# First attention layer: value products in half units behind a score group, a ring of four turned tiles, and another order of scores, copies and exponentials

## The reference

```
q, k, v = x @ Wq, x @ Wk, x @ Wv
attn = softmax((q @ k^T) * scale)     # per head, 512 x 512
out = (attn @ v) @ Wo
```

## Time and profile before

| what | us |
|---|---|
| median of three runs | 1487.92 |
| lowest, highest | 1484.96, 1489.2 |
| the profiled execution, its own time | 1479.72 |
| span of the profiled execution | 1477.9 |
| PE busy in the span | 1278.4 (87%) |
| DVE, ACT, POOL busy | 1058.7 (72%), 775.1 (52%), 524.5 (35%) |
| first and last score group begin | 21.4, 777.5 |

### The profile page before, as it was taken

How to read it: one execution, slowest core, us unless ns; L and a number is a source line. 1 busy time by engine, 2 the same in 40 slices (tenths; PEclk the granted TensorE clock), 3 DMA queues, 4 the chain that set the end, 5 groups by cost and what they waited for, 6 DMA issues and landing times. The chain is left out here.

```text
span 1477.9 us, 22423 instructions
## 1 busy us (share of the span) xinstructions
PE 1278.4 (87%) x8226; PEld 640.0 (43%) x8226; DVE 1058.7 (72%) x1823; ACT 775.1 (52%) x1308; POOL 524.5 (35%) x434
## 2 busy tenths in 40 slices
PE   4777788777877787877888899999999999999998
PEld 2232333232322233322333355585548654765466
DVE  6688877666766567656777498687878688669846
ACT  5676666554655557545661775236533554246532
POOL 2389853002210022100221156323733274317531
PEclk9899999998999999999999999999999999999999
DMA  7775545565555665565657502300230111210221
GB/s 242 187 168 99 92 91 90 105 123 104 92 104 98 130 114 98 106 119 114 112 102 227 212 20 55 86 16 29 55 71 23 37 45 43 55 37 19 55 48 44
DMA packets 346557, 135.52 MB, mean 92 GB/s; under 512 B 312176, under 2 KB 333392, under 8 KB 343888
## 3 DMA queue, kind: packets, MB, share of 16 engines
q1 hardware_dynamic: 334032, 132.52, 40.6%
q10 hardware_dynamic: 12416, 1.57, 1.0%
HBM read 44.87 MB, written 17.87 MB: 42 GB/s over the span
## 5 line engine op out<-in xcount | busy, mean ns | idle before, releaser
L929 ACT ACTIVATE probs<-vpair,top_n 128x512 f16<-128x512 f32 x256 | 164.4, 687 | 256.3 <-DVE top_n L627 256.3
L1143 PE MATMUL bank<-rows,both 128*128 128x512 f16 x1024 | 244.7, 392 | 5.2 <-DVE fd L700 4.1
L627 DVE TENSOR_REDUCE top_n<-vpair 128x1 f32<-128x512 f32 x256 | 164.5, 684 | 84.9 <-PE bank L1114 82.8
L443 POOL TENSOR_TENSOR h<-th,h 128x512 f16<-128x512 f32 x61 | 71.5, 1172 | 271.5 <-ACT h L898 271.5
L627 DVE TENSOR_REDUCE top_n<-bank 128x1 f32<-128x512 f32 x256 | 163.7, 681 | 0.0
L929 ACT ACTIVATE probs<-bank,top_n 128x512 f16<-128x512 f32 x256 | 162.6, 690 | 0.0
L1143 PEld LDWEIGHTS bank<-rows,both 128*128 128x128 f16 x1024 | 97.5, 100 | 144.5 <-issue 35.4
L2218 PE MATMUL bank<-rows,both 128*128 128x512 f16 x512 | 118.3, 382 | 0.0
L1114 PE MATMUL vpair<-qk 32*128 32x512 f16 x256 | 50.4, 389 | 74.4 <-ACT probs L929 74.4
L2234 PE MATMUL bank<-both,hid 128*128 128x512 f16 x512 | 111.2, 379 | 0.0
L1128 PE MATMUL bank<-probsT,vaug 128*32 128x512 f16 x512 | 45.3, 487 | 72.3 <-DMA probsT<-probs 60.4
(11 more groups left out here) (362 smaller groups left out, 2673.3 us busy)
## 6 DMA issues: line engine op xcount, KB each, us to landing
h<-in_ug SPq DMA_DIRECT2D x8, 1024.0 KB, 5.8
lt_scratch<-big SPq DMA_DIRECT2D x16, 384.0 KB, 2.7
dn<-in_down SPq DMA_DIRECT2D x2, 2048.0 KB, 11.1
x_scratch<-th SPq DMA_DIRECT2D x16, 256.0 KB, 2.6
res<-x_scratch SPq DMA_DIRECT2D x16, 256.0 KB, 4.1
out_x<-res SPq DMA_DIRECT2D x16, 256.0 KB, 2.0
both<-in_w SPq DMA_DIRECT2D x2, 1548.0 KB, 11.9
t_scratch<-tok SPq DMA_DIRECT2D x16, 192.0 KB, 2.1
```

What stands on the lines that cost most here:

```text
L443: pool.tensor_tensor(h16(ft, 1), row32, h16(ft, 0), ALU.subtract).then_inc(S["row_lo"], 1)
L627: v.tensor_reduce(top_n[:, i:i + 1], SC_[n % G][:, :], AX.X, ALU.max, negate=True).then_inc(S["max_done"], 1)
L929: a.activation(probs[:, k % TAKEN, j * T:(j + 1) * T], SC_[j][:, :], ACT.Exp, bias=top_n[:, i:i + 1]).then_inc(S["p_ready"], 1)
L1143: mm = pe.matmul(GB[n % 2][:, :], w[:, kt, col:col + P], xnb(b, kt), start=r == 0, stop=r == 2 * KT - 1)
```

## The change

- `weigh(n)` now forms the value products of two query tiles, 16 matmuls of 256 columns. It stands at t % 4 == 0, directly behind the score group of that step, and takes the tiles 2n and 2n + 1, whose scores stand eight and six steps before.
- `turn_probs(n)` waits only until the pair that held its quarter of `probsT` has been used: `probsT` becomes a ring of four turned tiles.
- `to_tokens`, `divide` and `to_features` move to the steps 4, 6 and, for the unit before last, 2.
- `load_heads` is split: k rows two units ahead at t % 8 == 6, q rows one unit ahead at t % 8 == 2.
- On PE, `scores` comes behind the turns and transforms of its step, and in the feed-forward stages behind a few of the step's matmuls: 4 or 3 of the gate stage (t % 4 == 0 or 2), 1 or 0 of the down stage.
- On ACT, `high_rows` and `high_half` come ahead of the exponentials of their step; the copies of q, v and k come one step later from t = 70 on.

```
-PV_STEP, TOKEN_STEP, DIVIDE_STEP, TURN_BACK = 2, 3, 4, 6
+TOKEN_STEP, DIVIDE_STEP, TURN_BACK = 4, 6, 2
+GATE_AHEAD, DOWN_AHEAD = (4, 3), (1, 0)
+LATE_EVICT = 70
...
+            def load_q(u):
+
+                slot = u % SLOTS
                 sp.wait_ge(S["mb_took"], MB["q", u // 2] + 1)
+                if u >= SLOTS:
+                    sp.wait_ge(S["s_ps"], (u - SLOTS + 1) * SC)
...
                 sp.wait_ge(S["p_ready"], G * (n + 1))
                 if u:
-                    sp.wait_ge(S["pv_done"], u)
+                    sp.wait_ge(S["pv_done"], n // 2 - 1)
...
-                if t % STEPS == STEPS - 2 and 1 < t // STEPS + 2 < NU:
-                    load_heads(t // STEPS + 2)
+                if t % STEPS == 6 and t // STEPS + 2 < NU:
+                    load_k(t // STEPS + 2)
+                if t % STEPS == 2 and 1 < t // STEPS + 1 < NU:
+                    load_q(t // STEPS + 1)
...
-                if t % STEPS == TURN_BACK and 0 <= t // STEPS - 1 < NU and t // STEPS % 2 == 0:
-                    to_features(t // STEPS - 1)
+                if t % STEPS == TURN_BACK and 0 <= t // STEPS - 2 < NU and t // STEPS % 2:
+                    to_features(t // STEPS - 2)
...
+                if t > FFN_STEP + 1 and (t - 2) // BSTEPS < B and (t - 2) % BSTEPS >= FFN_STEP and t % 2 == 0:
+                    high_rows((t - 2) // BSTEPS, ((t - 2) % BSTEPS - FFN_STEP) // 2)
                 if b < B and m > FFN_STEP and m % 2:
                     tanh_gate(b, (m - FFN_STEP) // 2)
+                if 0 <= t - PREP - 2 < NCH * KT:
+                    high_half(t - PREP - 2)
                 if t < NU * STEPS:
                     exps(2 * t)
                     exps(2 * t + 1)
...
-                if t % 16 == Q_STEP + 1 and t // 16 + 1 < NU // 2:
+                late = 1 if t < LATE_EVICT else 2
+                if t % 16 == Q_STEP + late and t // 16 + 1 < NU // 2:
                     evict_q(t // 16 + 1)
-                if m == K_STEP + 1 and b + 1 < B:
+                if m == K_STEP + late and b + 1 < B:
                     evict_k(b + 1)
...
-            def weigh(u):
-
+            def weigh(n):
+
+                u, half = divmod(n, 2)
                 b, g = divmod(u, NKV)
-                for i in range(TAKEN):
-                    pe.wait_ge(S[f"pt_in{i}"], 16 * ((TT * (u + 1) - 1 - i) // TAKEN + 1))
-                if u:
+                for k in (2 * n, 2 * n + 1):
+                    pe.wait_ge(S[f"pt_in{k % TAKEN}"], 16 * (k // TAKEN + 1))
+                if u and half == 0:
                     pe.wait_ge(S["o_free"], u)
-                if g == 0:
+                if g == 0 and half == 0:
                     pe.wait_ge(S["mb_took"], MB["v", b] + 1)
+                cols = slice(2 * P * half, 2 * P * (half + 1))
                 for kt in range(TT):
                     for j in range(G):
-                        mm = pe.matmul(OB[32 * j:32 * j + 32, :], vaug[:, b % 2, kt, g, :], probsT[:, TT * j + kt, :],
+                        mm = pe.matmul(OB[32 * j:32 * j + 32, cols], vaug[:, b % 2, kt, g, :], probsT[:, TT * j + kt, cols],
                                        start=kt == 0, stop=kt == TT - 1)
                 mm.then_inc(S["pv_done"], 1)
...
+            def ffn(t, first, last):
+
+                b, m = t // BSTEPS, t % BSTEPS
+                if b and m < FFN_STEP:
+                    for i in range(first, min(last, 6)):
+                        down_mm((b - 1) * TT + m // 8, 2 * (m % 8) + i // 3, i % 3)
+                if b < B and m >= FFN_STEP:
+                    for r in range(first, last):
+                        ffn_mm(b, m - FFN_STEP, r)
...
-                if t < NU * STEPS and t % 2 == 0:
-                    scores(t // 2)
-                if t % STEPS == PV_STEP and 0 <= t // STEPS - 1 < NU:
-                    weigh(t // STEPS - 1)
                 if t in TURN_STEP:
                     turn_x(KT + TURN_STEP.index(t))
                 if 0 <= t - PREP - 2 < NCH * KT:
                     transform_ug(t - PREP - 2)
+                ahead = 0
+                if t % 2 == 0:
+                    ahead = (DOWN_AHEAD if m < FFN_STEP else GATE_AHEAD)[t // 2 % 2]
+                ffn(t, 0, ahead)
+                if t < NU * STEPS and t % 2 == 0:
+                    scores(t // 2)
+                if t % 4 == 0 and 0 <= t // 4 - 2 < 2 * NU:
+                    weigh(t // 4 - 2)
+                ffn(t, ahead, 2 * KT)
```

More of the change, by code:

```diff
@@ L298, in _, with load_k @@
             load_chunk(1)
-            def load_heads(u):
+            def load_k(u):
                 b, g, slot = u // NKV, u % NKV, u % SLOTS
@@ L330, in load_raw @@
                 if i == 0:
-                    sp.wait_ge(S["pv_done"], NU)
+                    sp.wait_ge(S["pv_done"], 2 * NU)
                 if i == 2:
@@ L343, in turn_probs @@
                 if u:
-                    sp.wait_ge(S["pv_done"], u)
+                    sp.wait_ge(S["pv_done"], n // 2 - 1)
                 sp.dma_start_transpose(probsT[:, :, qt * P:(qt + 1) * P], probs[:, n % TAKEN, :]).then_inc(S[f"pt_in{n % TAKEN}"], 16)
-            load_heads(0)
-            load_heads(1)
+            for u in range(2):
+                load_k(u)
+                load_q(u)
             sp.dma_start(wsd[:, :], d["wscale_dp"].partition_broadcast(P)).then_inc(S["wo_in"], 16)
@@ L660, in to_tokens @@
             def to_tokens(u):
-                v.wait_ge(S["pv_done"], u + 1)
+                v.wait_ge(S["pv_done"], 2 * (u + 1))
                 if u:
@@ L917, in evict_v @@
                 if b >= 2:
-                    a.wait_ge(S["pv_done"], (b - 1) * NKV)
+                    a.wait_ge(S["pv_done"], 2 * (b - 1) * NKV)
                 a.activation(vaug[:, b % 2, :, :, 0:DH], MISC[:, :].rearrange("p (t g c) -> p t g c", t=TT, g=NKV),
@@ L989, in _ @@
                     evict_x(KT + TURN_STEP.index(t))
-                if 0 <= t - PREP - 2 < NCH * KT:
-                    high_half(t - PREP - 2)
                 for ft in range(FT):
@@ L996, in _ @@
                     high_down(DN_AT.index(t))
-                if t % 16 == Q_STEP + 1 and t // 16 + 1 < NU // 2:
+                late = 1 if t < LATE_EVICT else 2
+                if t % 16 == Q_STEP + late and t // 16 + 1 < NU // 2:
                     evict_q(t // 16 + 1)
-                if m == V_STEP + 1 and b + 1 < B:
+                if m == V_STEP + late and b + 1 < B:
                     evict_v(b + 1)
-                if m == K_STEP + 1 and b + 1 < B:
+                if m == K_STEP + late and b + 1 < B:
                     evict_k(b + 1)
-                if t > FFN_STEP + 1 and (t - 2) // BSTEPS < B and (t - 2) % BSTEPS >= FFN_STEP and t % 2 == 0:
-                    high_rows((t - 2) // BSTEPS, ((t - 2) % BSTEPS - FFN_STEP) // 2)
                 if b and m - 1 in DOWN_END:
@@ L1145, in ffn_mm, with down_mm @@
                     mm.then_inc(S["gb_full"], 1)
-            def down_mm(n, j):
+            def down_mm(n, j, r):
                 k, ft = GO["down", n], DN_TURN[j]
-                if j == 0:
+                if j == 0 and r == 0:
                     pe.wait_ge(S["gb_took"], k - 1)
-                if n % TT == 0:
+                if n % TT == 0 and r == 0:
                     pe.wait_ge(S["row_lo"], n // TT * FT + ft + 1)
-                if n == 0:
+                if n == 0 and r == 0:
                     pe.wait_ge(S["mb_took"], MB["dn", j] + 1)
                 bk, rows = GB[k % 2][:, :], slice(n % TT * P, (n % TT + 1) * P)
[L1157 to L1160, removed]
+                mm = pe.matmul(bk, h16(ft, r // 2)[:, rows], dn16(ft, r % 2), start=j == 0 and r == 0, stop=j == FT - 1 and r == 2)
+                if j == FT - 1 and r == 2:
                     mm.then_inc(S["gb_full"], 1)
+            def ffn(t, first, last):
[6 more added lines that the diff above has]
+                        ffn_mm(b, m - FFN_STEP, r)
             def turn_next():
@@ L1208, in _ @@
                     transform_dn(DN_AT.index(t))
[L1209 to L1214, removed]
                 if t % 16 == Q_STEP and t // 16 + 1 < NU // 2:
```

## The result

The changed kernel takes 1390.93 us (median of four runs, 1388.45 to 1393.41) against 1486.66 of the kernel before (four runs, 1484.96 to 1489.2): a ratio of 0.9355, 95% interval 0.9332 to 0.9378. It is faster by about 96 us; forecast were 108. The profiled execution of before was a low one of its kind (1479.72), that of after (1391.33) a typical one, so the traces show 88.4 us of the difference: 87.1 up to the last score group (777.5 to 690.37), 1.4 behind it.

The account below looks back on a forecast made before the run. No engine is saturated except POOL from 77 to 139 us; PE waits for turned tiles, and ACT's order costs too. Savings of 61 + 41.6 + 5 + 7.5 - 6.7 - 0.7 = 107.7 us give 1372 profiled, 1380 median; range 1360 to 1420.

Parts of the forecast that it names:

- first four units: First stage, 117.46 us before: 5 us less, bounds 0 and 8; POOL bounds from 77 us on.
- units 4 to 7: Stage of 104.00 us before, half still following POOL: 7.5 us less, bounds 0 and 14, ahead of load waits.
- tail: End of the kernel: 0.7 us more, as `to_tokens` comes behind DVE's weight maxima.
- The wait for the turned tiles: PE's stall at `weigh`: goes as a whole, tiles needing 5.5 of 7.3 us of lead in down stages.
- the margin of 1.8 us in down stages: Down stages: time to spare when a turned tile needs 5.5 us of the 7.3 us lead.
- The halves: PE's value products: each 256-column half takes 0.75 us, so a unit pays 1.5 for 1.05 us.
- Down units: Down stages: 16.25 us a unit, 65 a stage; three stages 195 for 256.1 before, 61 us less.
- Gate units: Gate stages: groups of 4.7 and 4.5 us, 18.5 a unit, 80.5 a stage; 41.6 us less over three.
- The ring through `gate_mul`: Gate groups: PE enters the next gate bank only after tanh and `gate_mul`, at S + 3.73 us, S being the scores.
- The split loads: Copy of k near m = 50 waits for the last q load: 1.6, 1.6 and 3.5, 6.7 us more.
- Rival (a): Gate and down stages after batch 0: turned tiles still late, 48 half products wait 1 us each, 1428 us; chance 0.19.
- rival (b): Two points per unit: a waiting half product holds the whole chain; slower kernel, 1524 us at 3 us each; chance 0.03.

Follow-up runs that it names:

- e8_loads: The changed kernel with a unit's k and q rows loaded together at step 6, as before the change; 1397.93 us, ratio 0.943.
- e6_ahead: The changed kernel with no feed-forward matmul ahead of a score group; 1371.71 us, ratio 0.9248.
- e4_halves: The kernel before with only halved value products two groups behind, the ring of four and later token steps, other orders as before; 1384.02 us, ratio 0.9339.
- e2_act: The changed kernel with ACT's high half behind the exponentials and the copy of xnT again, PE's order staying changed; 1382.92 us, ratio 0.9328.
- e1_pe: The changed kernel with PE's score group and value products ahead of the step's turns and transforms again; 1391.91 us, ratio 0.9395.
- e5_lead: The changed kernel with each half of the value products one score group earlier, leaving one group of lead; 1412.09 us, ratio 0.9523.
- e11_late: The changed kernel with the copies of q, v and k one step after their projection throughout, as before; 1408.71 us, ratio 0.9477.

## Why the prediction was right, and where not

The time, 1390.93, lies in the range and close to the forecast of 1380; the main mechanism is shown. A part of the closeness is luck: by the profiled executions the forecast was 1372, against 1391.33, and the 8.2 us added for the low execution of before closed some of the gap. Term by term, by the profiled executions:

| term | forecast | measured |
|---|---|---|
| three down stages, 256.1 before | 195 | 197.9 |
| three gate stages, 278.5 before | 236.8 + 3.2 of waits | 236.3 |
| first four units | 5 less | 19.7 more, 3.6 of it ahead of the first group |
| units 4 to 7, 104.0 before | 4.0 less | 6.4 less |
| tail | 0.7 more | 1.4 less, with layer 1 |

*The wait for the turned tiles* goes as a whole, as forecast: in the changed kernel all value products together wait 0.2 us for a turned tile, and no idle time of PE's matmuls ahead of them, whatever it is booked to, is longer than 0.42 us. Its causes were the lead and the loads ahead of the turn on SP; what the single space added is not separated from halves and orders (12 of 58 us in the down stages, with them). I had named all three, and the margin of 1.8 us in down stages was right to the extent that taking 2.5 us of it away (`e8_loads`) brings small waits back.

*The halves* cost 0.55 us each, near the lower bound of 0.52, not 0.75. So a unit pays 1.10 for 1.05. The drain that the Trainium skill puts on a change of tiling mode (TensorEngine Tiling (Array Packing), Tiling Modes) is not separable in these rows: 16 matmuls of 256 columns, four side by side, stream for 0.43 us (four times half of 0.217, an estimate from the spacing of the 512-column matmuls), and all that is left for drains and weight loads together is 0.12.

*Down units* 14.8 to 18.5 us, 16.0 on average in two stages: right. The first down stage, 69.7, still has the last transforms of the down weights in its first unit (20.91 us), which I did not price.

*Gate units*: 19.3 in place of 18.5, with fewer extras than assumed. The ring through `gate_mul` was read rightly, except that a transpose of DVE stands ahead of it in one group of each unit (`to_tokens`, 4.91 us) and in a second one of every other unit (`to_features`, 5.12 us). Gate groups of 4.83 or more through `gate_mul` were named as a sign of being wrong, and these are such groups. What I took from it was wrong in one respect: I let the matmuls ahead of the scores pass as a filler, though my own lines had the chain at 4.31 and the group with them at 4.7. `e6_ahead` shows the difference as the price, 3.5 us a stage. Most of the gain of the gate stages (37.9 of 42.2 us) comes with the halves and the removed stall: with `e4_halves` they take 240.6 in place of 278.5.

*The step that failed is the first four units*: "the new order may cost or bring some 3", since "POOL bounds from 77 on, so only what comes before counts". POOL bounded a stretch whose PE and ACT had slack; the changed orders used up more than the slack. The prediction gave both moves together one guess of 3 us and did not follow one step around both queues; either move alone costs 14 to 22 us at the end of unit 3 (`e2_act`, `e1_pe`). That this stretch might grow, by transforms that hold up the scores, it did name as a sign of being wrong. A check from rows of before was possible: a turn step then costs a copy 0.6, a turn 0.2, a transform 1.9, a high half 0.7 and two exponentials 1.2, 4.6 us in series, 9.2 for a group with turns in both steps, against the 6 to 6.6 us of most groups there. Measured, the two groups with turns in both steps of units 1 and 2 take 11.3 and 12.3 us, and those with one turn 6.4 to 9.4 there. So the sum gives the direction and not the full size.

*The split loads*: the wait of the copy of k was foreseen, at 1.6 us in two batches and 3.5 in batch 0; it is 1.2 and free in the two, for the late copy meets ACT's idle time, and 1.3 in batch 0, where it costs 1.4. Its price without the late copy (6.3 and 6.8 us) I would have missed.

Rival (a), turned tiles still late, did not happen; rival (b), two points per unit that hand a wait on to the whole chain, is real as a mechanism, as 2.2 to 2.9 us waits cost 4 to 6 us in `e5_lead` and `e11_late`, but nothing there waits in the changed kernel.

## What to carry to other kernels

Give a consumer of a transfer as much lead as issue, queue and landing take together, and a ring deep enough to allow it: with the products in halves, that was worth the whole gain here. Before instructions are moved on two engines at once, follow one iteration around both queues and add up what is in series; either of two moves can close a ring by itself, and undoing one of them then shows little of what it costs. And idle time ahead of the instruction that closes the critical chain is no gap to be filled: work put there moves the chain behind the work's own waits.

## What the runs showed of the hardware

A transposing transfer of a 128 x 2048 tile of two-byte values occupies SP for 1.3 to 3.4 us in the down stages, in the median 1.93 before and 2.19 after. It lands 4.4 us after the issue starts before and 4.5 after (medians; the longest takes 6.1 and 6.2), though the DMA engines' share in the down stages rose to 0.81.

Idle time of PE in otherwise dense work costs more than it lasts, because the granted clock falls to 1.2 GHz. Before, 21 waits ahead of value products between 242 and 778 us lasted 1.5 us or more (1.57 to 4.73); during or within 3 us behind 19 of them the clock was at 1.2 GHz, and behind two, of 1.86 and 2.86 us, it stayed full (the second is the wait at 522.23 in the earlier trace rows). In `e5_lead`, between 242 and 712 us, two of seven waits of 1.6 to 2.3 us were followed by it, in `e11_late` both of 3.9 to 4.0 us. While it lasts, a score matmul takes 0.60 us in place of 0.39 and a half 1.04 in place of 0.62. In the changed kernel, whose longest such idle time of PE is 1.62 us, the clock was 1.00 in every stage from 256 us on.
